# Routing places computed on GpSimd, and the channel product of the search rounds in rounded parts

## The chip, the cores and the metric

One core of a Trainium2 chip runs the whole kernel. The metric is the device time of one execution in microseconds (us). Engines are named as the profile names them: PE is TensorE, DVE VectorE, ACT ScalarE, POOL GpSimd, SP the queue that issues most plain DMAs. A semaphore is a counter; each engine works through its own instructions in order and waits where the program says so.

## What is computed

The input is 8192 tokens of 256 channels. Each is normalised (`xn`); then two branches are multiplied:

```python
s = rwkv(xn)      # k, v, r = mixes @ Wk, Wv, Wr; a recurrence over time; x += (sigmoid(r) * att) @ Wo
                  # kf = square(relu(xk2 @ WfkT)); s = x + sigmoid(xr2 @ WfrT) * (kf @ WfvT)
probs = softmax(xn @ Wg)                       # 8 experts
top_idx = top_k(probs.T, tokens // 8)          # each expert's 1024 tokens
expert = argmax over the experts that took the token, or over all if none did
g = silu(prob of the expert * gelu(xn @ W1[expert]) @ W2[expert])
out = x + s * g
```

`Wfv` is 1024 x 256: the second channel product `kf @ WfvT` sums over 8 chunks of 128.

## The kernel before

**Rounds.** The tokens go in 16 rounds (b = 0 to 15) of 512, four tiles (j) of 128. Round b runs three things woven together: the recurrence and the output projection of block b, the projections of block b + 1, and the channel mixing of block b - 1. Each engine has a written order, one function `round_` per engine; most rounds are hardware loops.

PE's round: `hidden(b - 1)` (8 chunks h into three PSUM banks, in rounded parts already: a high and a low part of weights and data in F32R, three products in place of one float32 product), `receptance(b - 1)`, `turn1(b + 1)`, `channel_out(b - 1, 0)`, `project_out(b)`, a routing step, `project(b + 1, 0, 1)`, `channel_out(b - 1, 1)`, `turn2(b)`, a routing step, `project(b + 1, 2)`, `channel_out(b - 1, 2)`, a routing step, `channel_out(b - 1, 3)`. `channel_out(b, j)` (line 961) is a tile's 8 products in float32, one per chunk, 128x128 weights from `kf2` and 256 columns of `wfv`:

```python
for h in range(HC):
    ins = pe.matmul(psKV[:, j // 2, ...], kf2[:, h, j * P:(j + 1) * P], wfv[:, h, :], start=(h == 0), stop=(h == HC - 1))
```

ACT's round (line 665): `logs`, `relu` and `square` of the first chunks (lines 642, 646), `shares(b)` (lines 626, 629; waits for DVE's `wkv_gap`), more `relu`, `norm1(b + 1)` (line 545, waits for POOL's `rstd1`), the last `relu` and `square`, `affine1`, `sigmoid_fr`, `take_kvr` in pieces (lines 590, 592), `norm2`, `affine2`, exponents, and `split_mix`, which makes `mix_hi`.

DVE's round: `wkv_state` (scans, line 1453), `embed_scale` and `embed_shift` of b + 1 (1558, 1563), routing point 0, `wkv_gap` (1460), `gate_out(b - 2)` (1542), `moments1(b + 1)` (1375, 1379), `residual2(b - 2)` (1549), `wkv_mix` (1471 to 1500), routing point 1, `mix1(b + 1)` (1392, 1396), `residual1(b)` (1533, waits for the output projection) with its statistics, point 2, `mix1_r`, `wkv_start` (1439 to 1447), point 3, `mix2` (1392, 1396, and 1431, which waits for `mix_hi`).

POOL's round: `rstd1(b + 1)` and `rstd2(b)`, four instructions on 128x4 each (lines 441 to 446), which turn variances into scales. `norm_scales` does the same for the first normalisation in rounds 0 to 3 (lines 409 to 425).

**Routing.** The logits and the softmax are made in rounds 0 to 3. In the search rounds 4 to 10 DVE looks bit by bit for each expert's threshold, four bits a round, one at each point (`try_bit`, lines 1210 to 1217: compare 128x512 and count; PE adds over partitions, line 837). Round 11 (`SELECT_ROUND`) counts ties, selects and chooses. In round 12 (`LIST_ROUND`), point 0, `place_tokens` (lines 1294 to 1347) turns the prefix sums (`win`), the counts (`psR`) and the one-hot choice (`pexp`), all 128x512, into a place for each token, and makes `expert_at`, the expert of each of the MLP's tiles. `routed` then frees SP, which loads W2 into the desk (a buffer whose upper part holds the routing tables; its lower 4096 words hold inputs of the router's rounds and nothing in the search rounds). SP then stores `s`, copies rows of x, loads the list, and W1.

**The list.** `list_part` (1354, 1355) copies 16 tiles' places and rows each round from 12 to 15, because the instruction in a loop needs fixed addresses, and `add_to_list` issues 16 indirect DMAs a round (line 434), eight behind `rstd1` and eight behind `rstd2` (all sixteen ahead of `rstd2` in round 15).

**The MLP.** 71 tiles of 128 tokens, each with its expert's weights; the second product is in rounded parts, 128x128 weights by 256 columns (lines 1062 to 1064). It starts about 826 us into the span.

## Time and profile before

| | us |
|---|---|
| median of 3 runs | 1076.61 (1076.31 to 1077.09) |
| the profiled execution | 1077.64 |
| its span, first to last instruction | 1075.8 |
| PE busy / DVE busy | 1015.7 / 882.0 |
| ACT busy / POOL busy | 689.6 / 383.4 |
| mean granted clock of PE | 0.981 |

Busy time is the union of an engine's records in the span. PE's records overlap, and their ends are modelled, so a spacing is read from starts. A float32 product has two records, a rounded one (F32R) one. A granted clock of 1 is 2.4 GHz and 0.5 is 1.2 GHz.

### The profile page before, as it was taken

Reading aid. Unit: us, or ns where it says so; the run is one execution under the profiler, and the core shown is the slowest. Engines: PE = TensorE matmul, PEld = TensorE weight load, DVE = VectorE, ACT = ScalarE, POOL = GpSimd, SP = SyncE. Lnnn points to the kernel's source line nnn. Section 1 sums busy time; section 2 is a strip of 40 time slices with the busy share of each in tenths; the row PEclk is TensorE's granted clock in tenths of the full one; section 3 lists DMA queues with packets and bytes.
Section 4 is the critical chain, followed back from the end, with each engine's and each line's share of the span. In section 5 each row is a group of like instructions: output and inputs, shape, how many; then the busy total and the mean of one; then the engine's idle time right before and its main releaser. Section 6 shows DMA issues by size and latency. Waiting matters only on the chain.

```text
span 1075.8 us, 18544 instructions
## 1 busy us (share of the span) xinstructions
PE 1015.7 (94%) x5410; PEld 832.7 (77%) x5410; DVE 882.0 (82%) x1763; ACT 689.6 (64%) x1231; POOL 383.4 (36%) x407
## 2 busy tenths in 40 slices
PE   4899999899999999999999969999999999999996
PEld 4578787677777767777776757777788999999996
DVE  5899898998988889898899987887665777777775
ACT  2558567585857658585765557595555666666663
POOL 3204055110101021010101045656762776666663
PEclk9889999999999999999999989999999999999998
DMA  7544320101102010110101020124361433333320
GB/s 257 168 141 120 98 79 20 40 7 54 58 0 58 0 58 15 43 58 0 58 0 59 1 59 1 59 68 129 120 223 40 122 122 114 113 114 109 108 67 21
DMA packets 59473, 80.28 MB, mean 75 GB/s; under 512 B 7678, under 2 KB 46719, under 8 KB 59394
## 3 DMA queue, kind: packets, MB, share of 16 engines
q1 hardware_dynamic: 48130, 54.16, 15.9%
q0 software_dynamic: 11280, 25.32, 7.9%
q8 instruction: 35, 0.57, 0.2%
q14 instruction: 28, 0.23, 0.1%
HBM read 64.38 MB, written 26.36 MB: 84 GB/s over the span
## 4 chain that ended last, share of the span: by engine, by line
PE 59%; DVE 19%; issue 9%; ACT 7%; POOL 4%; DMA 1%; DVEq 1%; SPq 0%; ACTq 0%; POOLq 0%
PE psKV L968 12%; PE psM L1042 11%; PE psM L905 11%; PE psM L919 5%; DVE arena L1453 2%; DVE arena L1396 2%; ACT arena L646 2%; PE psT L870 2%; ACT arena L545 2%; DVE bnst L1375 2%; PE psM L937 2%; PE psM L956 2%; PE psKV L1062 2%; POOL cf L444 2%; PE psKV L1064 1%
## 5 line engine op out<-in xcount | busy, mean ns | idle before, releaser
L968 PE MATMUL psKV<-arena 128*128 128x256 f32 x1024 | 231.2, 380 | 2.6 <-ACT arena L646 2.6
L968 PEld LDWEIGHTS psKV<-arena 128*128 128x128 f32 x1024 | 192.7, 190 | 42.0 <-issue 17.5
L441 POOL TENSOR_SCALAR lnw<-mv 128x4 f32<-128x4 f32 x32 | 19.0, 593 | 519.2 <-DVE mv L1379 519.2
L1042 PE MATMUL psM<-arena 128*128 128x128 f32 x1136 | 139.5, 276 | 1.5 <-DVE arena L1630 1.4
L1042 PEld LDWEIGHTS psM<-arena 128*128 128x128 f32 x1136 | 132.2, 192 | 3.2 <-DVE arena L1630 2.5
L937 PE MATMUL psM<-mix_hi,wfk_hi 128*128 128x512 f32 x256 | 107.8, 421 | 21.2 <-ACT arena L642 21.2
L592 ACT ACTIVATE arena<-psM 128x512 f32<-128x512 f32 x64 | 36.5, 588 | 127.9 <-PE psM L905 127.9
L1396 DVE SCALAR_TENSOR_TENSOR arena<-arena,vecs 128x512 f32<-128x512 f32 x160 | 109.9, 745 | 0.1
L507 POOL DMA_INDIRECT out_dram<-arena,list_sb x71 | 86.5, 1218 | 59.1 <-DVE arena L1661 50.4
L545 ACT ACTIVATE arena<-s_ring,cf 128x256 f32 (+1 forms) x128 | 66.4, 591 | 59.9 <-POOL cf L446 59.9
L939 PE MATMUL psM<-mix_hi,wfk_lo 128*128 128x512 f32 x256 | 102.3, 400 | 0.0
L642 ACT ACTIVATE arena<-psM 128x512 f32<-128x512 f32 x128 | 73.7, 587 | 28.9 <-PE psM L944 26.4
L768 ACT ACTIVATE arena<-psM 128x512 f32<-128x512 f32 x71 | 42.5, 599 | 63.2 <-PE psM L1042 63.2
L434 POOL DMA_INDIRECT sorted_list<-info_cur,place_cur x64 | 73.7, 1151 | 22.3 <-issue 20.6
L944 PE MATMUL psM<-mix_lo,wfk_hi 128*128 128x512 f32 x256 | 80.9, 398 | 0.0
L937 PEld LDWEIGHTS psM<-mix_hi,wfk_hi 128*128 128x128 f32 x256 | 49.7, 194 | 36.5 <-ACT arena L642 26.8
L646 ACT ACTIVATE arena<-arena 128x512 f32<-128x512 f32 x128 | 75.2, 624 | 1.0
L494 POOL DMA_INDIRECT arena<-xs_rows,list_sb x62 | 65.9, 1063 | 21.0 <-issue 18.6
L956 PE MATMUL psM<-arena 128*128 128x256 f32 x256 | 60.4, 383 | 4.6 <-ACT arena L642 4.6
L905 PE MATMUL psM<-arena,wk 128*128 128x512 f32 x128 | 61.5, 626 | 0.5 <-DVE arena L1396 0.5
L919 PE MATMUL psM<-wo,arena 128*128 128x256 f32 x256 | 59.4, 386 | 0.7 <-DVE arena L1500 0.5
L1392 DVE TENSOR_TENSOR arena<-arena 128x512 f32<-128x512 f32 x64 | 41.7, 688 | 22.0 <-ACT arena L553 21.9
(212 smaller groups left out, 2368.4 us busy)
## 6 DMA issues: line engine op xcount, KB each, us to landing
arena<-in_x SPq DMA_DIRECT2D x16, 512.0 KB, 4.1
desk<-in_xT SPq DMA_DIRECT2D x16, 512.0 KB, 4.1
xs_rows<-s_ring SPq DMA_DIRECT2D x16, 512.0 KB, 3.2
xs_rows<-in_x SPq DMA_DIRECT2D x16, 512.0 KB
desk<-in_x SPq DMA_DIRECT2D x15, 512.0 KB, 5.0
desk<-in_W SPq DMA_DIRECT2D x8, 512.0 KB, 8.4
arena<-in_W SPq DMA_DIRECT2D x8, 512.0 KB, 7.3
out_dram<-arena,list_sb POOLq DMA_INDIRECT x71, 2.7
```

The source lines that it names most:

```text
L507: pool.indirect_dma_start(out[:, :], bass.IndirectOffsetOnAxis(list_sb[:, t, 0:1], axis=0), out_t[i], None, bounds_check=T - 1, oob_is_err ...
L545: ins = act.activation(hn[:, j], xs[:, j * C:(j + 1) * C], ACT.Identity, scale=cf[:, 0, j:j + 1], bias=cf[:, 1, j:j + 1])
L646: act.activation(kf2[:, h], kf2[:, h], ACT.Square).then_inc(S["sq_done"], 1)
L905: ins = pe.matmul(psM[:, u % 3, :], w[:, k, c * P:(c + 1) * P], mixA[:, m, k, :], start=(k == 0), stop=(k == CH - 1))
L919: ins = pe.matmul(psM[:, 1 + j // 2, (j % 2) * C:(j % 2 + 1) * C], att[:, c, j * P:(j + 1) * P], wo[:, c, :], start=(c == 0), stop=(c == C ...
L937: pe.matmul(psM[:, h % 3, :], wfk_hi[:, k, n], mix_hi[:, k, :], start=(k == 0), stop=False)
L939: pe.matmul(psM[:, h % 3, :], wfk_lo[:, k, n], mix_hi[:, k, :], start=False, stop=False)
L944: ins = pe.matmul(psM[:, h % 3, :], wfk_hi[:, k, n], mix_lo[:, k, :], start=False, stop=(k == CH - 1))
L956: ins = pe.matmul(psM[:, (HC + u) % 3, (j % 2) * C:(j % 2 + 1) * C], mixB_r[:, k, j * P:(j + 1) * P], wfr[:, k, :], start=(k == 0), stop=( ...
L968: ins = pe.matmul(psKV[:, j // 2, (j % 2) * C:(j % 2 + 1) * C], kf2[:, h, j * P:(j + 1) * P], wfv[:, h, :], start=(h == 0), stop=(h == HC ...
L1042: ins = pe.matmul(psM[:, t % 2, f * P:(f + 1) * P], w1_t[t % 2][:, k, f * P:(f + 1) * P], xnT[t % 2][:, k, :], start=(k == 0), stop=(k == ...
L1396: return v.scalar_tensor_tensor(dst[:, c], dmix[:, c], vecs[:, c, V[m]:V[m] + 1], hT[:, c, 0:SEQ], ALU.mult, ALU.add)
```

## The change

Two things. The places are computed by four passes of POOL over 128x512 between DVE's steps, over the tables themselves; the list is scattered from `place` and `info` directly, in unrolled rounds; `expert_at` is made in round 14. And in rounds 4 to 11 `channel_out` becomes `channel_part`: by pairs of chunks p in place of tiles, from high and low parts. ACT makes `kf_hi` (two slots of two chunks, in the desk) and `wfv_hi`, POOL makes `kf_lo` and `wfv_lo` in the place of `kf2` and `wfv`. Ahead of round 12 POOL adds `wfv` together again. On ACT squares 4 to 7 move behind `affine1`.

POOL:

```diff
-            def add_to_list(b, half):
-
-                wait_run(pool, S["list_cur"], b - (LIST_ROUND - 1))
-                if isinstance(b, int) and b == LIST_ROUND:
...
+                for t in range(first, last):
+                    pool.indirect_dma_start(sorted_list[:, :], bass.IndirectOffsetOnAxis(place[:, t:t + 1], axis=0),
+                                            info[:, t, :].bitcast(I32), None).then_inc(S["list_scattered"], 16)
 
             def rstd(b, stats, mv, lnw, cf, step, ready):
 
...
+            def place_in_lists():
+
+                st = Steps(pool, S["place_step"], 4, 0, S["waited"])
+                pool.wait_ge(S["counts_kept"], 1)
+                pool.wait_ge(S["route_step"], R_KEPT)
+                st.then(pool.tensor_tensor(by_tile(before), by_tile(before), by_expert(counts), ALU.subtract))
+                pool.wait_ge(S["route_step"], R_STARTS)
+                st.wait()
+                st.then(pool.tensor_tensor(by_tile(before), by_tile(before), by_expert(work), ALU.add))
+                st.wait()
...
+                st.wait()
+                st.then(pool.tensor_tensor(before, before, chosen, ALU.mult))
+                st.end()
+
+            def take_lo(b, p):
+                wait_run(pool, S["kf_hi_done"], (b - BIT_ROUND) * J + (p + 1))
+                n, slot = slice(2 * p, 2 * p + 2), 2 * (p % 2)
+                pool.tensor_tensor(kf_lo[:, n], kf2[:, n], kf_hi[:, slot:slot + 2].bitcast(F32), ALU.subtract
...
+            def split_wfv():
+                pool.wait_ge(S["wfv_hi_done"], 1)
+                pool.wait_ge(S["kv_done"], J * ROUTER_ROUNDS)
+                pool.tensor_tensor(wfv_lo, wfv, wfv_hi.bitcast(F32), ALU.subtract).then_inc(S["wfv_lo_done"], 1)
+
+            def join_wfv():
+                pool.wait_ge(S["kv_done"], J * SELECT_ROUND)
+                pool.tensor_tensor(wfv, wfv_lo.bitcast(F32), wfv_hi.bitcast(F32), ALU.add).then_inc(S["wfv_whole"], 1)
+
+            def parts_round(b):
+                rstd1(b + 1)
+                take_lo(b, 0)
+                take_lo(b, 1)
+                rstd2(b)
+                take_lo(b, 2)
+                take_lo(b, 3)
+
+            def round_(b, mid=(0, 0), late=(0, 0), ahead=True):
                 if ahead:
                     rstd1(b + 1)
-                if listing:
-                    add_to_list(b, 0)
-                if not ahead:
-                    add_to_list(b, 1)
+                if isinstance(b, int) and b == LIST_ROUND:
+                    pool.wait_ge(S["pads_out"], 16)
+                    pool.wait_ge(S["route_step"], R_PLACED)
+                add_to_list(*mid)
                 rstd2(b)
                 if not ahead:
                     zero_rows()
-                if listing and ahead:
-                    add_to_list(b, 1)
+                add_to_list(*late)
 
...
-            norm_scales(ROUTER_ROUNDS + 1, NB - 4, NB - 1)
-            with pool.Fori(ROUTER_ROUNDS, LIST_ROUND) as b:
-                round_(b)
-            round_(LIST_ROUND, listing=True)
-            with pool.Fori(LIST_ROUND + 1, NB - 1) as b:
-                round_(b, listing=True)
-            round_(NB - 1, listing=True, ahead=False)
+            norm_scales(ROUTER_ROUNDS + 1, NB - 4, NB - 2)
+            norm_scales(ROUTER_ROUNDS + 2, NB - 1, NB - 1)
+            round_(ROUTER_ROUNDS)
+            split_wfv()
+            with pool.Fori(BIT_ROUND, LIST_ROUND) as b:
+                parts_round(b)
+            join_wfv()
+            place_in_lists()
+            round_(LIST_ROUND, mid=(0, 4), late=(4, 17))
+            round_(LIST_ROUND + 1, mid=(17, 26), late=(26, 39))
+            round_(LIST_ROUND + 2, mid=(39, 48), late=(48, 60))
+            round_(NB - 1, mid=(60, NTILE), ahead=False)
 
```

ACT:

```diff
+            def take_hi(b, p):
+                act.wait_ge(S["sq_done"], b * HC + (2 * p + 2))
+                act.wait_ge(S["kv_done"], b * J + (p - 1))
+                slot = 2 * (p % 2)
+                act.activation(kf_hi[:, slot:slot + 2], kf2[:, 2 * p:2 * p + 2], ACT.Copy).then_inc(S["kf_hi_done"], 1)
...
+            def split_wfv():
+                act.wait_ge(S["logits_done"], NB)
+                act.wait_ge(S["a_step"], 2 * NB)
+                act.activation(wfv_hi, wfv, ACT.Copy).then_inc(S["wfv_hi_done"], 1)
...
-            def round_(b, ffn=True, ahead=True, softmax=False, further=True):
+            def keep_counts():
+                act.wait_ge(S["route_pe"], 4)
+                act.activation(logits.rearrange("p (e t) -> p e t", e=E), psR[:].rearrange("p (t e) -> p e t", e=E),
...
                     relus(b - 1, 5)
+                if parts:
+                    take_hi(b - 1, 0)
                 if ahead:
                     norm1(b + 1)
                 if ffn:
                     relus(b - 1, 6)
                     squares(b - 1, 3)
                     relus(b - 1, 7)
-                    squares(b - 1, 4, 5, 6, 7)
+                    if not parts:
+                        squares(b - 1, 4, 5, 6, 7)
                 if softmax:
                     act.wait_ge(S["route_exp_in"], 1)
                     act.activation(probs, logits, ACT.Exp).then_inc(S["route_exp_out"], 1)
                 if ahead:
                     affine1(b + 1)
+                if softmax:
+                    split_wfv()
                 if isinstance(b, int) and b == 1:
                     keep_logits(2)
                 if ffn:
...
                     act.activation(wfk_hi[:], wfk, ACT.Copy).then_inc(S["wfk_hi_done"], 1)
+                if parts:
+                    squares(b - 1, 4, 5)
+                    take_hi(b - 1, 1)
                 if ahead:
                     take_kvr(b + 1, 0, 2)
                 if not ffn:
                     keep_logits(1)
+                if parts:
+                    squares(b - 1, 6, 7)
+                    take_hi(b - 1, 2)
                 norm2(b)
                 if ahead:
                     take_kvr(b + 1, 2, 4)
...
                 affine2(b)
                 if ahead:
                     exp_past(b + 1)
+                    if parts:
+                        take_hi(b - 1, 3)
                     take_kvr(b + 1, 4, 5)
                     exponents(b + 1)
                 split_mix(b, 0)
...
             round_(ROUTER_ROUNDS, softmax=True)
-            with act.Fori(BIT_ROUND, NB - 2) as b:
+            with act.Fori(BIT_ROUND, LIST_ROUND) as b:
+                round_(b, parts=True)
+            round_(LIST_ROUND, placing=True)
+            with act.Fori(LIST_ROUND + 1, NB - 2) as b:
                 round_(b)
             round_(NB - 2, further=False)
             round_(NB - 1, ahead=False)
```

PE:

```diff
-            def round_(b, extra, ffn=True, ahead=True):
+            def channel_part(b, p):
+                if p == 0:
+                    pe.wait_ge(S["wfv_lo_done"], 1)
+                    wait_run(pe, S["s_mult"], b)
+                done = b * J - (BIT_ROUND - 1) * J + (p + 1)
+                pe.wait_ge(S["kf_hi_done"], done)
+                out = lambda j: psKV[:, j // 2, (j % 2) * C:(j % 2 + 1) * C]
+                for j in range(J):
+                    for h in (2 * p, 2 * p + 1):
+                        hi = kf_hi[:, h % 4, j * P:(j + 1) * P]
+                        pe.matmul(out(j), hi, wfv_hi[:, h, :], start=(h == 0 and j % 2 == 0), stop=False)
+                        pe.matmul(out(j), hi, wfv_lo[:, h, :], start=False, stop=False)
+                pe.wait_ge(S["kf_lo_done"], done)
+                for j in range(J):
+                    for h in (2 * p, 2 * p + 1):
+                        ins = pe.matmul(out(j), kf_lo[:, h, j * P:(j + 1) * P], wfv_hi[:, h, :],
+                                        start=False, stop=(h == HC - 1 and j % 2 == 1))
+                ins.then_inc(S["kv_done"], 1)
+
+            def round_(b, extra, ffn=True, ahead=True, channel_out=channel_out):
                 if ffn:
                     hidden(b - 1, extra, b)
                     receptance(b - 1)
...
                 round_(b, router_point)
             round_(ROUTER_ROUNDS, softmax)
             with pe.Fori(BIT_ROUND, SELECT_ROUND) as b:
-                round_(b, sum_bit)
-            round_(SELECT_ROUND, route)
+                round_(b, sum_bit, channel_out=channel_part)
+            round_(SELECT_ROUND, route, channel_out=channel_part)
+            pe.wait_ge(S["wfv_whole"], 1)
             with pe.Fori(LIST_ROUND, NB - 1) as b:
                 round_(b, nothing)
             round_(NB - 1, nothing, ahead=False)
...
```

DVE (the eight lines of `place_tokens` from the reduction on stay):

```diff
                 elif point == 0:
+                    expert_starts()
+                elif point == 1:
                     place_tokens()
...
+            def expert_starts():
+                v.wait_ge(S["counts_kept"], 1)
+                R.then(v.tensor_tensor_scan(work, reset, logits, 0.0, ALU.mult, ALU.add))
+                R.wait()
+                R.then(v.tensor_scalar(starts(0).bitcast(I32), et(work)[:, :, NTILE - 1], float(P - 1), None, ALU.add))
+                R.wait()
+                R.then(v.tensor_scalar(starts(1).bitcast(I32), starts(0).bitcast(I32), 7, None, ALU.logical_shift_right))
+                R.wait()
+                R.then(v.tensor_copy(starts(2), starts(1).bitcast(I32)))
+                R.wait()
+                R.then(v.tensor_tensor_scan(starts(3), ones[:, 0:E], starts(2), 0.0, ALU.mult, ALU.add))
+                R.wait()
+                R.then(v.tensor_tensor(starts(4), starts(3), starts(2), ALU.subtract))
+                R.wait()
+                R.then(v.tensor_scalar(starts(5), starts(4), float(P), -1.0, ALU.mult, ALU.add))
...
-                R.then(v.tensor_tensor(work, work, logits, ALU.subtract))
-                R.wait()
-                R.then(v.tensor_tensor(et(work), et(work), c8(5).rearrange("p (e o) -> p e o", o=1).to_broadcast([P, E, NTILE]),
-                                       ALU.add))
-                R.wait()
-                R.then(v.tensor_tensor(te(win), te(win), work.rearrange("p (e t) -> p t e", e=E), ALU.add))
-                R.wait()
-                R.then(v.tensor_tensor(win, win, pexp, ALU.mult))
-                R.wait()
+                v.wait_ge(S["place_step"], 4)
...
                 R.then(v.tensor_scalar(info[:, :, 1:2].rearrange("p t o -> p (t o)"), gate, 0.5, None, ALU.mult))
+                R.wait()
+                assert R.k == R_PLACED, R.k
+
+            def tile_experts():
...
                 R.then(v.tensor_reduce(win[0:1, 0:NT], tw3, AX_X, ALU.add))
                 R.wait()
...
                 v.tensor_copy(tiny[:, 60:61], tiny[:, 0:1]).then_inc(S["routed"], 1)
                 R.end()
...
-            def list_part(b):
-
-                n = b - LIST_ROUND
-                if not (isinstance(b, int) and b == LIST_ROUND):
-                    wait_run(v, S["list_scattered"], n * (16 * LT))
-                v.tensor_copy(place_cur[:], place[:, ds(n * LT, LT)])
-                v.tensor_copy(info_cur[:].rearrange("p t w -> p (t w)"),
-                              info[:].rearrange("p t w -> p (t w)")[:, ds(n * (4 * LT), 4 * LT)].bitcast(I32)
-                              ).then_inc(S["list_cur"], 1)
-
             def listing(b, point):
-                if point == 0:
-                    list_part(b)
+                if point == 2 and isinstance(b, int) and b == NB - 2:
+                    tile_experts()
 
 
```

## Rows read from the trace of the kernel before

**Rows 1.** The page, part 1: busy us, share, instructions.

```profile
PE 1015.7 (94%) x5410; PEld 832.7 (77%) x5410; DVE 882.0 (82%) x1763; ACT 689.6 (64%) x1231; POOL 383.4 (36%) x407
```

**Rows 2.** Table by stretches: stretch: length, busy by engine, granted clock, DMA.

```profile
483.65:530.55 46.90, 45.41 (x192) 34.24 (x193) 41.23 (x86) 32.13 (x55) 5.47 (x8) 1.00 0.11 34
577.96:632.56 54.60, 44.56 (x169) 32.76 (x170) 51.81 (x99) 29.25 (x49) 7.09 (x10) 0.91 0.07 21
632.56:677.88 45.32, 44.27 (x185) 33.40 (x185) 36.33 (x64) 30.64 (x52) 24.67 (x25) 1.00 0.12 35
```

**Rows 3.** Waits of DVE, 202 to 578 us: total us, times, longest.

```profile
DVE s_ring L1533 <- PE psM L919: 14.1, 8, 2.0
DVE desk L1210 <- PE psR L837: 7.9, 8, 1.4
```

**Rows 4.** Chain of waits in the search rounds: start, us, what.

```profile
451.00 3.45 PE psKV L968 x16
```

**Rows 5.** Timeline of PE in the MLP: start, us, instruction.

```profile
899.77 0.28 PE L1062 MATMUL psR<-w_hi,hT_h 128*128 x1
...
900.72 0.28 PE L1064 MATMUL psR<-w_hi,hT_l 128*128 x1
```

**Rows 6.** Groups by line on ACT, 483.65 to 530.55 us: busy, mean ns | idle before.

```profile
L592 ACT ACTIVATE arena<-psM 128x512 f32<-128x512 f32 x4 | 2.2, 586 | 8.0 <-PE psM L905 8.0
...
L603 ACT ACTIVATE arena<-arena 128x1024 f32<-128x1024 f32 x1 | 1.1, 1052 | 0.0
```

**Rows 7.** Groups by line and shape on POOL, whole span.

```profile
L458 POOL MEMSET arena<- 128x512 f32 x9 | 4.2, 523 | 0.0
...
L413 POOL TENSOR_TENSOR desk<-desk,info 128x12 f32<-128x12 f32 x1 | 0.2, 223 | 0.1
...
L422 POOL TENSOR_TENSOR stats<-desk,info 128x4 f32<-128x4 f32 x1 | 0.2, 201 | 0.1
```

**Rows 8.** Timeline of DVE and POOL at 520 us.

```profile
520.22 1.22 DVE L1549 TENSOR_TENSOR s_ring<-s_ring,arena 128x1024 f32 x1
...
520.33 1.17 POOL L441 TENSOR_SCALAR lnw<-mv 128x4 f32<-128x4 f32 x1 [23.61 <-DVE mv L1379]
```

**Rows 9.** Single lines, whole span: count: ns min/median/max, first and last start.

```profile
L441 POOL TENSOR_SCALAR lnw<-mv x32: 192/385/1172, 19.5 to 779.1; 128x4 f32<-128x4 f32 x32
...
L442 POOL TENSOR_SCALAR lnw<-mv x32: 192/267/1667, 19.8 to 779.4; 128x4 f32<-128x4 f32 x32
...
L1630 DVE COPY arena<-arena x71: 681/685/885, 795.5 to 1058.4; 128x1024 f32 x71
...
L1396 DVE SCALAR_TENSOR_TENSOR arena<-arena,vecs x160: 718/746/754, 27.6 to 788.4; 128x512 f32<-128x512 f32 x160
```

**Rows 10.** Groups by line on DVE, 483.65 to 530.55 us.

```profile
L1217 DVE TENSOR_SCALAR_CACHE_REDUCE desk<-desk 128x512 f32<-128x512 f32 x4 | 3.0, 746 | 0.7 <-DVE desk L1215 0.7
L1375 DVE BATCH_NORM_STATS2 bnst<-s_ring 128x6 f32 x8 | 2.8, 415 | 0.1
```

**Rows 11.** Timeline of DVE in the placing round.

```profile
611.66 0.68 DVE L1297 COPY desk<-psR 128x512 f32<-128x512 f32 x1
...
618.02 0.69 DVE L1324 TENSOR_REDUCE desk<-desk 128x64 f32<-128x512 f32 x1
...
619.88 0.74 DVE L1339 TENSOR_TENSOR desk<-desk 1x576 f32<-1x576 f32 x1
...
621.89 1.28 DVE L1460 TENSOR_TENSOR arena<-arena 128x512 f32<-128x512 f32 x2
```

**Rows 12.** Timeline of PE in the placing round: idle before it in brackets.

```profile
627.07 0.80 PE L937 MATMUL psM<-mix_hi,wfk_hi 128*128 128x512 f32 x1 [10.03 <-ACT arena L642]
```

**Rows 13.** Table by stretches behind PE's idle time.

```profile
627.10:632.56 5.46, 5.46 (x13) 4.31 (x14) 5.46 (x10) 4.48 (x9) 4.43 (x6) 0.50 0.67 200
```

**Rows 14.** POOL: group of the list's issues, and timeline behind the last.

```profile
L434 POOL DMA_INDIRECT sorted_list<-info_cur,place_cur x64 | 73.7, 1151 | 22.3 <-issue 20.6
...
779.13 0.19 POOL L441 TENSOR_SCALAR lnw<-mv 128x4 f32<-128x4 f32 x1 [1.04 <-DVE mv L1379]
```

52 lines of the change are left out of this document (26 added, 26 removed).

## The prediction

> **What bounds the kernel now.** The page comes first: TensorE (PE) is busy 94% of the span, VectorE (DVE) 82%, ScalarE (ACT) 64%, GpSimd (POOL) 36% [rows 1]. Such shares mix stages, so the table by stretches is next. The search rounds, from one first channel product (`channel_out`, j = 0) to the next, repeat every 46.90 us with PE busy 45.41 and DVE 41.23. A round without routing work takes 45.32 with PE busy 44.27. The stretch of the select round and the placing takes 54.60 with PE busy only 44.56 at a mean granted clock of 0.91 and DVE busy 51.81 [rows 2]. So plain rounds are PE's; in a search round both engines are almost full; in the placing stretch DVE is the bound.
>
> How much of a search round's DVE is free? Its waits on other engines say it: over eight rounds 14.1 us for the output projection and 7.9 us for the bit's sum [rows 3], so 1.8 + 1.0 = 2.8 us per round. What DVE needs for itself is 46.9 - 2.8 = 44.1 us (41.2 busy, the rest dispatch between dependent instructions). PE needs 45.4. A change that takes work from PE can gain until DVE's 44.1 are reached, and anything over 2.8 us per round put on DVE lengthens the round.
>
> **The change, part by part.**
>
> *Channel product in parts, rounds 4 to 11.* Now a quarter of it is 16 records in 3.45 us (two for each of 8 products of 128x256) [rows 4]: 13.8 us per round. The new form is 96 single products with rounded operands. The MLP has that shape: eight steps from 899.77 to 900.72, 0.119 us each, weight load included [rows 5]. 96 x 0.119 = 11.4: PE gets 2.4 us shorter, to 43.0, below DVE's 44.1. Were nothing else changed, the round would fall to about 44.3, by 2.6 us.
>
> *ACT, per round.* `take_hi` adds four copies of 128x1024, 1.05 us each (nearest row, an Exp of that size) = 4.2 us. ACT waits 8.0 us per round for the projection [rows 6] and is busy 32.1 of 46.9 [rows 2]. The first copy lies ahead of `norm1`, where it waits for POOL's scales today. The second and third, with the squares moved there, lie around the first two `take_kvr`, where the 8.0 are. The fourth delays `exponents` and `split_mix` by 1.05, and DVE reaches `mix_lo` about when `mix_hi` ends today: up to 0.3 us. I take 0 to 0.3 per round. Without these gaps it would be 4.2.
>
> *POOL, per round.* `take_lo` adds four subtractions of 128x1024, both inputs in SBUF. No row has such a pass. Below: 512 words are written in 0.52 us by a memset [rows 7], 1.02 ns each; at that rate a pass of 1024 is 1.05. Above: undisturbed two-input operations take 0.201 us for 4 elements and 0.223 for 12 [rows 7], 2.75 ns an element, so 3.0. I take two streams read one after the other at the memset's rate, 1024 x 2 x 1.02 = 2.1 us. GPSIMD Engine Reference of the Trainium skill (section 3.1) gives 4497 ns for an add of 2048, which would make it 2.25; no run here has shown it.
>
> POOL itself has the time (5.5 of 46.9 busy [rows 2]), and by the order on the engines PE asks for each low part 5 to 10 us after its high part is made. What counts is DVE. A POOL instruction on 4 elements takes 0.192 us at its shortest and 1.172 at its longest [rows 9]; a long one begins at 520.33 inside a DVE add of two SBUF operands (520.22 for 1.22) and ends 0.06 behind it [rows 8]. POOL waits for the rest of DVE's whole instruction. Does it hold the other way too? A DVE copy of 128x1024 takes 0.685 at the median and up to 0.885 beside POOL's issues, but `mix` never more than 0.754 against 0.746 in 160 [rows 9]: the reads of POOL have been too small to tell. I take it that it does, for the pass's whole 2.1 us: the wait seen is for a complete instruction, and that is a lock and not a shared rate.
>
> The Trainium skill states that lock for both sides: SBUF — State Buffer, section Who interferes with whom, says that a DVE instruction with two SBUF inputs and a POOL instruction that reads SBUF exclude each other, and that whichever issues first keeps the port to its end. The rows above agree for one direction. By that rule the sum is the one below; by the `mix` row alone (DVE never held) it would be rival one's.
>
> Not all of DVE competes: statistics (2.8), the counting pass (3.0) [rows 10], the two operations with a PSUM operand and small ones leave about 10 of 44 us free of it. So a pass costs DVE 0.77 x 2.1 = 1.6, four 6.5. Round: 44.1 + 6.5 = 50.6, +3.7. Seven steady rounds: **+26**. In round 11 DVE has no slack to give: **+6.5**; PE's saving there gains nothing.
>
> *Splitting the weights.* `split_wfv`: 2048 wide, 4.2 us on POOL at the start of round 4, beside scans of DVE: 0.77 x 4.2 = **+3** (bounds 0 and 5.6); the copy on ACT, twice 1.05, is in its gap.
>
> *Joining them and placing, round 12.* Today the placing runs from 611.66 to 621.89 on DVE, ahead of `wkv_gap` [rows 11]; ACT stands in `shares` behind it and PE idles 10.03 us for the next `relu` [rows 12], then runs 5.5 us at a granted clock of 0.50, its lower level, 1.2 GHz [rows 13]: 2.7 lost. After, point 0 keeps the scan and six small ones, 1.2 + 6 x 0.2, so 2.5 us at most: 7.7 less. Of these, the part from the reduction at 618.02 to 619.88 returns behind `wkv_mix` (1.9), the tiles' experts up to 621.89 in round 14 (2.0), where DVE has 36.3 of 45.3 busy [rows 2]. The counts' copy goes to ACT (0.6, ahead of `relu`: nothing). But `join_wfv`, 2048 wide, may start only when round 11's last product is done, and PE waits for it before its next instruction: 4.2 us of PE idle, and DVE held at its scans for 0.77 x 4.2 = 3.2. The four placing passes of 512 (1.05 each) hold DVE another 3, about half ahead of `wkv_gap`. DVE reaches the gap 7.7 - 3.2 - 1.5 = 3.0 earlier, and some of the clock's loss goes with it, less what the first norm behind these passes on POOL is late. **-3** (bounds -8, with DVE never held, and +4, where the join delays all).
>
> *The list.* 64 issues stay, 1.15 us each [rows 14]. The two small copies per round and the wait for landed parts go; in round 15 twelve issues fewer lie ahead of `rstd2`. POOL idles 1.04 us between its last issue and that norm today [rows 14], so this gives nothing. `routed` comes in round 14 instead of 12. SP waits for it in order, with W2's loads, a store of `s`, five copies of x, the list's load and W1's behind it; SP gets there only after its loop, in round 14, so it is late by less than half a round, and W2 is first read behind round 15's hidden product: 0. The list's own load waits for the last scatter as before. `norm_scales` of the last block is split, one short set more on POOL, idle there: 0.
>
> Sum: 26 + 6.5 + 3 - 3 = **+32** on the profiled execution's 1077.64, its span of 1075.8 plus 1.8 around it: 1109.6. The median of the runs is 1.0 lower: **1109 us**. With passes of 1.05 it is 44.1 + 3.2 = 47.3, +0.4 x 7 + 3.2 + 1.6 - 5 = +3: 1079. With passes of 3.0 that all meet a competing instruction, 44.1 + 12 = 56.1, +9.2 x 7 + 12 + 6 + 4 = +86: 1163. Both ends need every unknown at once; I take 1083 to 1132 as the forecast's own range.
>
> **Rivals.** *One: DVE is not held* (for: the `mix` row; against: the wait for a whole instruction, [rows 8, 9]). Then seven rounds gain 2.6 (18), round 11 nothing, the placing 6 to 8: 1076.6 - 25 = 1052, from 1048 to 1060. It ends on the other side. The point that decides is the hold of one pass: at 2.8 / (4 x 0.77) = 0.9 us the round is as long as before. Chance 0.33.
> *Two: POOL loses every contest*, and the low parts come late. DVE keeps 44.1, but PE waits at `kf_lo`; the fourth part has the least room, 5 us. A wait of 2 to 3 us per round gives back what PE saved: 1070 to 1090, say 1077. For it: another small POOL instruction has taken 1.667 us [rows 9], more than any one DVE instruction beside it. Against: the wait at 520.33 ended at the next boundary [rows 8]. Chance 0.08.
> *Three: the parts don't save PE time* (with operands that alternate, steps nearer 0.144, where 96 take 13.8) while DVE is held as forecast: 1113, inside the forecast's range, chance 0.04.
> The forecast itself has 0.55.
>
> **How the numbers follow.** About 0.2% (2 us) is what this measurement can tell from no change. Slower: the forecast and three 0.59, less 0.02 for its low end, and 0.04 of rival two, 0.61. Faster: rival one and 0.02 of rival two, 0.35. The same: 0.04. To hold eight in ten the range has to reach from rival one's middle to the forecast's upper end: 1050 to 1130.
>
> **What would show it.** Right: in the search rounds DVE's two-input instructions (`mix`, scans of 1.2 us) with records or gaps of 2 to 3 us wherever POOL has a `take_lo`, rounds of about 50 us, PE busy about 43 of them, DVE never waiting for the output projection. PE idle 4 us at the head of round 12. Wrong: `mix` still 0.75 beside POOL's passes and rounds of 44 to 45 us; or POOL's passes at 1 us; or PE waiting for POOL at the parts.

## The result, and the profile after

| | before | after |
|---|---|---|
| median, us (lowest to highest) | 1076.46 (1075.79 to 1077.09) | 1120.62 (1120.22 to 1121.17) |
| span of the profiled execution | 1075.8 | 1119.2 |
| mean granted clock | 0.981 | 0.969 |

The medians are of 4 runs each. The ratio is 1.041 [1.039, 1.043]: 44 us slower. The forecast was 1109, 32 us slower, with 1050 to 1130 as the range. That range reaches from 26 us faster to 54 us slower; the forecast's own 1083 to 1132 is the narrower test, and it holds the result too.

The first part of the page after the change, to be read against [rows 1]:

```profile
PE 1016.1 (91%) x5666; PEld 835.0 (75%) x5666; DVE 951.9 (85%) x1750; ACT 720.4 (64%) x1265; POOL 493.0 (44%) x455
```

DVE is busy 70 us longer on work that has fewer instructions than before (1750 in place of 1763). PE is busy as long as before, though its products became fewer microseconds. Both need the stages. Here are stretches of the changed kernel, each from the start of one `residual2` on DVE to the next: a search round, the select round with the join and the placing, and the round behind it.

```profile
core 0: us, PE busy (x) PEld busy (x) DVE busy (x) ACT busy (x) POOL busy (x), PEclk, DMA share, GB/s
502.34:554.74 52.40, 45.65 (x224) 34.54 (x224) 49.62 (x87) 35.81 (x59) 16.72 (x12) 0.97 0.10 30
607.73:671.89 64.16, 49.60 (x225) 37.15 (x226) 63.37 (x88) 37.99 (x62) 26.94 (x17) 0.92 0.08 25
671.89:715.75 43.86, 42.23 (x176) 31.61 (x176) 38.28 (x73) 28.71 (x50) 27.51 (x25) 1.00 0.13 37
```

The search round went from 46.90 to 52.40 us and DVE from 41.2 to 49.6 busy. The starts of `residual2` in the rounds split the difference between the two spans, 43.4 us:

| from the `residual2` of one round to that of another | before | after | difference |
|---|---|---|---|
| round 2 to 3 | 50.76 | 48.83 | -1.9 |
| 3 to 4 (with `split_wfv`) | 46.35 | 50.09 | +3.7 |
| 4 to 11, seven search rounds | 328.90 | 367.49 | +38.6 |
| 11 to 12 (last parts, join, placing) | 58.20 | 64.16 | +6.0 |
| 12 to 13 | 45.98 | 43.86 | -2.1 |
| 13 to the end | 403.9 | 403.5 | -0.4 |

The rows add up to +43.9; ahead of round 2 the changed kernel gains another 0.4.

**What stretches DVE.** The timeline of the changed kernel in one search round, POOL's four `take_lo` (line 484) and the DVE records beside them. Columns: start, duration, engine, line, operation, tiles, shapes, and how many instructions the row joins.

```profile
506.53 3.32 POOL L484 TENSOR_TENSOR kf_lo<-arena,kf_hi 128x1024 fp32r<-128x1024 f32 x1
517.08 2.69 POOL L484 TENSOR_TENSOR kf_lo<-arena,kf_hi 128x1024 fp32r<-128x1024 f32 x1 [7.23 <-ACT kf_hi L699]
528.32 2.44 POOL L484 TENSOR_TENSOR kf_lo<-arena,kf_hi 128x1024 fp32r<-128x1024 f32 x1 [0.42 <-ACT kf_hi L699]
537.25 2.83 POOL L484 TENSOR_TENSOR kf_lo<-arena,kf_hi 128x1024 fp32r<-128x1024 f32 x1 [6.48 <-ACT kf_hi L699]
...
507.61 3.39 DVE L1567 SCALAR_TENSOR_TENSOR arena<-arena 128x512 f32<-128x512 f32 x2
517.48 4.82 DVE L1480 SCALAR_TENSOR_TENSOR arena<-arena,vecs 128x512 f32<-128x512 f32 x4
528.43 4.53 DVE L1523 TENSOR_TENSOR_SCAN arena<-wneg,arena 128x512 f32<-128x512 f32 x2
537.73 4.89 DVE L1480 SCALAR_TENSOR_TENSOR arena<-arena,vecs 128x512 f32<-128x512 f32 x4
```

Beside no pass, the same rows take 1.28 (line 1567, two instructions), 2.73 (line 1480, four) and 2.33 (the scans, two). The differences are 2.11, 2.09, 2.20 and 2.16: one DVE instruction in each row stood still for about 2.1 us. So it is with all 32 passes of rounds 4 to 11: each held one DVE instruction with two SBUF inputs. Which one changes from round to round: a scan (lines 1562, 1523), `mix` (1480) or one of the operations beside them (1567, 1476, 1527), in round 11 also one of the selection. One line's own statistics say it too: minimum, median, maximum.

```profile
L1480 DVE SCALAR_TENSOR_TENSOR arena<-arena,vecs x160: 720/745/2899, 27.0 to 832.1; 128x512 f32<-128x512 f32 x160
```

Before, `mix` never took more than 0.754 [rows 9]. With 4 x 2.14 = 8.6 taken off, the round is 43.8, DVE's own need (44.1 in the prediction).

**Who waits now.** The waits of DVE, then of PE, in the search rounds after the change (202 to 606): who, for whom, in total, times, the longest.

```profile
DVE desk L1311 <- PE psR L918: 1.4, 1, 1.4
DVE s_ring L1617 <- PE psM L1000: 0.4, 1, 0.4
```

```profile
PE psM L1018 <- ACT arena L689: 23.8, 14, 3.2
PE psM L986 <- DVE arena L1480: 16.6, 7, 2.6
```

DVE's 14.1 us for the output projection and 7.9 for the bit's sum [rows 3] are gone: 0.4 and 1.4, once each, is all that it still waits for PE. PE waits for `mix`, and for the `relu` on ACT that stands behind DVE's work. Such a wait costs PE twice, as idle time and as a slower clock behind it. PE's timeline at the end of one:

```profile
499.18 0.40 PE L1018 MATMUL psM<-mix_hi,wfk_hi 128*128 128x512 f32 x1
499.42 0.40 PE L1020 MATMUL psM<-mix_hi,wfk_lo 128*128 128x512 f32 x1
...
503.17 0.65 PE L1018 MATMUL psM<-mix_hi,wfk_hi 128*128 128x512 f32 x1 [2.90 <-ACT arena L689]
503.62 0.63 PE L1020 MATMUL psM<-mix_hi,wfk_lo 128*128 128x512 f32 x1
504.04 0.63 PE L1018 MATMUL psM<-mix_hi,wfk_hi 128*128 128x512 f32 x1
```

Ahead of the idle 2.90 us the starts are 0.23 apart, behind it 0.43, until 506.6: the granted clock went from its upper level (2.4 GHz) to its lower one (1.2 GHz). That is why PE is busy 45.65 in this round, not the 43.0 forecast. PE being late, though, moved nothing here, as DVE was later still.

**The weights' split and join.** The timeline of the changed kernel around `split_wfv` (line 490), and around `join_wfv` (line 494):

```profile
229.54 5.18 POOL L490 TENSOR_TENSOR wfv_lo<-arena,wfv_hi 128x2048 fp32r<-128x2048 f32 x1 [17.03 <-PE psKV L1049]
...
230.51 4.23 DVE L1314 TENSOR_TENSOR desk<-desk 128x1 f32<-128x1 f32 x1
234.89 0.16 DVE L1316 TENSOR_TENSOR desk<-desk 128x1 int32<-128x1 int32 x1
```

```profile
652.16 4.88 POOL L494 TENSOR_TENSOR arena<-wfv_lo,wfv_hi 128x2048 f32<-128x2048 f32 x1 [1.35 <-PE psKV L1068]
...
652.61 5.59 DVE L1515 TENSOR_TENSOR mix_lo<-arena,mix_hi 128x512 fp32r<-128x512 f32 x2
...
657.64 0.77 PE L1018 MATMUL psM<-mix_hi,wfk_hi 128*128 128x512 f32 x1 [5.56 <-POOL arena L494]
```

The split shows the hold at its purest: a DVE operation on one element per partition (two inputs, both in SBUF), 0.159 us at the median of its 29 occurrences, took 4.23 and ended at 234.74, where POOL's pass ended (234.72). The join held `mix_lo` for 5.59 - 1.28 = 4.3 us and PE for 5.56.

### The profile page after: what moved, and what is told of

Read it like the earlier page. It is cut to its first block, busy times and chain, and to the rows that moved or that the text cites. A ratio compares the mean times of both kernels' runs of the same rounds, so it can differ in the third digit from the quotient of the medians.

```text
span 1119.2 us, 19095 instructions
## 1 busy us (share of the span) xinstructions
PE 1016.1 (91%) x5666; PEld 835.0 (75%) x5666; DVE 951.9 (85%) x1750; ACT 720.4 (64%) x1265; POOL 493.0 (44%) x455
## 4 chain that ended last, share of the span: by engine, by line
PE 51%; DVE 27%; issue 12%; ACT 5%; POOL 3%; DVEq 1%; DMA 1%; SPq 0%; ACTq 0%; POOLq 0%
PE psM L1143 11%; PE psKV L1049 7%; PE psM L986 6%; DVE arena L1480 5%; PE psM L1000 4%; PE psM L1037 3%; DVE bnst L1459 2%; DVE arena L1537 2%; PE psM L1018 2%; PE psM L1025 2%; PE psM L1020 2%; DVE arena L1523 2%; PE psKV L1163 1%; PE psKV L1165 1%; PE psKV L1164 1%
## 5 line engine op out<-in xcount | busy, mean ns | idle before, releaser
L484 POOL TENSOR_TENSOR kf_lo<-arena,kf_hi 128x1024 fp32r<-128x1024 f32 x32 | 91.8, 2870 | 122.1 <-ACT kf_hi L699 122.1
L1480 DVE SCALAR_TENSOR_TENSOR arena<-arena,vecs 128x512 f32<-128x512 f32 x160 | 139.6, 930 | 0.1
L1049 PE MATMUL psKV<-arena 128*128 128x256 f32 x512 | 114.5, 380 | 0.5 <-ACT arena L693 0.5
L1049 PEld LDWEIGHTS psKV<-arena 128*128 128x128 f32 x512 | 96.8, 190 | 18.7 <-issue 6.3
L1020 PE MATMUL psM<-mix_hi,wfk_lo 128*128 128x512 f32 x256 | 105.9, 414 | 0.0
L438 POOL DMA_INDIRECT sorted_list<-info,place x64 | 74.3, 1161 | 28.3 <-issue 18.5
L986 PE MATMUL psM<-arena,wk 128*128 128x512 f32 x128 | 68.1, 677 | 19.9 <-DVE arena L1480 19.1
L1025 PE MATMUL psM<-mix_lo,wfk_hi 128*128 128x512 f32 x256 | 84.4, 412 | 1.1 <-DVE mix_lo L1515 1.1
L600 ACT ACTIVATE arena<-psT,vecs 128x512 f32<-128x512 f32 x64 | 46.2, 772 | 39.1 <-PE psT L951 35.5
L1063 PE MATMUL psKV<-wfv_hi,kf_hi 128*128 128x256 f32 x256 | 69.8, 313 | 0.0
```

The source lines that it names most:

```text
L438: pool.indirect_dma_start(sorted_list[:, :], bass.IndirectOffsetOnAxis(place[:, t:t + 1], axis=0), info[:, t, :].bitcast(I32), None).then_ ...
L484: pool.tensor_tensor(kf_lo[:, n], kf2[:, n], kf_hi[:, slot:slot + 2].bitcast(F32), ALU.subtract).then_inc(S["kf_lo_done"], 1)
L986: ins = pe.matmul(psM[:, u % 3, :], w[:, k, c * P:(c + 1) * P], mixA[:, m, k, :], start=(k == 0), stop=(k == CH - 1))
L1020: pe.matmul(psM[:, h % 3, :], wfk_lo[:, k, n], mix_hi[:, k, :], start=False, stop=False)
L1025: ins = pe.matmul(psM[:, h % 3, :], wfk_hi[:, k, n], mix_lo[:, k, :], start=False, stop=(k == CH - 1))
L1049: ins = pe.matmul(psKV[:, j // 2, (j % 2) * C:(j % 2 + 1) * C], kf2[:, h, j * P:(j + 1) * P], wfv[:, h, :], start=(h == 0), stop=(h == HC ...
```

## The experiments

The first four ran on one chip (the kernel before: 1076.21), the next three on a second and the last three on a third, where the kernel before takes 1090.08 and 1088.93. The stretch behind the last `residual2` takes 267 to 269 us on these two and 254 on the first. So ratios and round lengths are compared between chips, not totals, and an expected total is read as its ratio to the 1076.5 that it was worked out from.

**Placing on its own.** The change without the parts: `round_` in place of `parts_round`, no split, no join, `channel_out` in every round.

```diff
-            split_wfv()
             with pool.Fori(BIT_ROUND, LIST_ROUND) as b:
-                parts_round(b)
-            join_wfv()
+                round_(b)
```

> The changed kernel with only its first half: places on POOL, the list from the tables, the split norm_scales; the channel product stays in float32 in all rounds. Theory (a POOL pass that reads SBUF holds DVE's two-input instructions for about 2.1 us per 1024 words): search rounds back at 46.9, nothing to join, and the placing gives what the chain of before promised: 7.7 us less ahead of wkv_gap, less some 1.5 to 3 of hold by the four passes of 512, and 2.4 from the split norm_scales: 1064 to 1070 us. Rival (the placing itself costs, the first norm being late on POOL behind it): 1074 or more.

Measured: 1065.31, ratio 0.989 [0.988, 0.991]. The placing part is a gain of 11 us, and the parts cost 55.

```profile
423.41:470.31 46.90, 45.40 (x194) 34.23 (x193) 41.23 (x87) 32.15 (x55) 5.48 (x8) 1.00 0.11 34
564.75:617.83 53.08, 47.75 (x197) 35.08 (x196) 50.68 (x89) 34.35 (x59) 12.56 (x12) 0.99 0.10 30
617.83:662.19 44.36, 44.36 (x176) 33.54 (x177) 38.26 (x73) 28.77 (x50) 27.51 (x25) 0.94 0.13 37
```

These are stretches of this kernel. The total is in the 1064 to 1070 expected. The search round is the old one to the hundredth; the select and placing stretch is 5.1 us shorter than the old 58.20, and the next 1.6. Against the same stretch of the full change (64.16, DVE 63.37) DVE is 12.7 less busy, about four holds (8.6) and the join's (4.3).

**Splitting `norm_scales` on its own**, in the kernel before.

```diff
-            norm_scales(ROUTER_ROUNDS + 1, NB - 4, NB - 1)
+            norm_scales(ROUTER_ROUNDS + 1, NB - 4, NB - 2)
+            norm_scales(ROUTER_ROUNDS + 2, NB - 1, NB - 1)
```

> The kernel before with norm_scales of the last block split off, nothing else. Theory: round 3 of the changed kernel began 2.4 us earlier than before because of this alone: 1074 us (1073.5 to 1075). Rival (the 2.4 us come from the weights' copy or from the other order on ACT): 1076.5.

Measured: 1074.13, ratio 0.9987 [0.9976, 0.9997]; the stretch from the `residual2` of round 2 to that of round 3 is 48.84 in place of 50.76. The prediction had put this edit at nothing; it gives 2 us, as this run's expectation had it. Where it comes from is one DVE row, before and with the edit (line 1171 is line 1170 of the kernel before):

```profile
186.40 0.69 DVE L1170 TENSOR_TENSOR desk<-desk,info 128x512 f32<-128x512 f32 x1 [2.92 <-POOL info L425]
183.60 0.69 DVE L1171 TENSOR_TENSOR desk<-desk,info 128x512 f32<-128x512 f32 x1 [0.93 <-POOL info L425]
```

DVE multiplies the logits by the scales and waits for POOL's last ones. Split, POOL does three quarters of that set in time that was idle before, and DVE waits 2.0 us less.

**The write alone**: a memset of the same words in place of `take_lo`. PE's third product is taken from the high part, so the low part of the data is left out of the result.

```diff
-                pool.tensor_tensor(kf_lo[:, n], kf2[:, n], kf_hi[:, slot:slot + 2].bitcast(F32), ALU.subtract
-                                   ).then_inc(S["kf_lo_done"], 1)
+                pool.memset(kf2[:, n], 0.0).then_inc(S["kf_lo_done"], 1)
```

> The changed kernel with take_lo a memset of the same 1024 words (written, nothing read), and PE's third product taken from the high part, so that the low part of kf is left out of the result; all waits, copies of ACT and PE's products stay. Theory (POOL's reads hold DVE): rounds of 44.3 to 45.5 us in place of 52.4, DVE's mix at 0.75 again: 1120.6 - 7 x 7.5 - 8.5 = 1060 (1055 to 1068). Rival (the rounds are long because of the order: ACT's four copies, the moved squares, PE waiting at the parts): over 50 us per round, above 1100.

Measured: 1062.63, ratio 0.987 [0.986, 0.989], rounds of 44.65, the later ones of 45.49, in each of which DVE waits 0.8 for the output projection. The group of these passes, then a round of this kernel:

```profile
L484 POOL MEMSET arena<- 128x1024 f32 x32 | 30.5, 952 | 142.7 <-ACT kf_hi L698 142.7
```

```profile
418.30:463.79 45.49, 42.66 (x224) 33.41 (x224) 41.41 (x86) 35.63 (x59) 9.21 (x12) 1.00 0.11 35
```

DVE's 41.4 is what it was before (41.2). So in the search rounds ACT's copies, PE's new products and POOL's writes lengthen nothing; the loss there goes with what the passes read.

**The subtractions on DVE**: POOL does none, DVE does all four at its routing points.

```diff
+                if parts:
+                    take_lo(b, 0)
```

(and so for 1, 2 and 3, with `v.tensor_tensor` in place of `pool.tensor_tensor`)

> The changed kernel with the four take_lo of a round done by DVE itself (1.22 us each by its rows of that size), at the places where POOL's passes would have been ready. Theory (a POOL pass costs DVE its read time, 2.1 us, more than the same work on DVE): rounds of 44.1 + 4.9 = 49.0 to 49.5: 1120.6 - 7 x 3.1 - 3.5 = 1095 (1090 to 1100). Rival (DVE is slowed only because it is full, POOL's pass takes work from it that it would otherwise do): the same or longer than the changed kernel, 1120 to 1135.

Measured: 1102.29, ratio 1.024 [1.020, 1.028], above the 1095 expected and outside its range; rounds of 49.5, but for three of 51.2 to 51.9. DVE is busy 45.6 a round, 4.4 more than before. The expectation had left out a wait of PE for the low parts, here from 240 to 540:

```profile
PE psKV L1064 <- DVE kf_lo L1655: 19.2, 12, 2.2
```

Two of a round's four parts come late in this way, and DVE waits in turn for the output projection, up to 2.8 us at a time. Even so, DVE doing the work itself is 18 us faster than DVE held while POOL does it.

**Two passes beside instructions that don't compete.** `take_lo` 0 waits for `gap_done`, 1 for `o_done` and `mix1_done`; `take_hi` 0 moves ahead of `shares`.

```diff
-                rstd1(b + 1)
+                wait_run(pool, S["gap_done"], b * CH + CH)
                 take_lo(b, 0)
+                rstd1(b + 1)
+                wait_run(pool, S["o_done"], b + 1)
+                wait_run(pool, S["mix1_done"], 2 * b + 4)
                 take_lo(b, 1)
```

> The changed kernel with take_lo 0 and 1 of each search round moved: pass 0 waits for gap_done, so that it lies beside gate_out (a PSUM operand) and the block's statistics, pass 1 waits for o_done and mix1_done, so that it lies beside residual1 (a PSUM operand), its statistics and the counting pass. Passes 2 and 3 stay, nothing is left out, and POOL's work is the same. If a pass holds DVE only where DVE's instruction reads two SBUF tensors, two of four holds of 2.1 us go: a round of 52.4 - 4.2 = 48.2, eight rounds 33 less, about 1087 (1080 to 1094), with no long statistics records. If any POOL pass holds any DVE instruction, or if the work as such counts, it stays at 1115 to 1121, with the long records on other lines.

Measured: ratio 1.017 [1.015, 1.020] against 1.041: about 26 of the 33 us expected, just outside the range (1.003 to 1.016 as a ratio). The timeline has POOL's two moved passes first, then DVE: beside the pass at 454.60, beside one that was left in place (469.82), and beside the pass at 484.12:

```profile
454.60 2.37 POOL L484 TENSOR_TENSOR kf_lo<-arena,kf_hi 128x1024 fp32r<-128x1024 f32 x1 [13.55 <-PE psM L1003]
...
484.12 2.37 POOL L484 TENSOR_TENSOR kf_lo<-arena,kf_hi 128x1024 fp32r<-128x1024 f32 x1 [11.96 <-DVE arena L1547]
...
454.34 1.22 DVE L1620 TENSOR_TENSOR s_ring<-s_ring,psM 128x1024 f32 x1 [1.56 <-PE psM L1003]
455.70 1.40 DVE L1462 BATCH_NORM_STATS2 bnst<-s_ring 128x6 f32 x4
...
469.82 4.88 DVE L1483 SCALAR_TENSOR_TENSOR arena<-arena,vecs 128x512 f32<-128x512 f32 x4
...
483.69 1.21 DVE L1629 SCALAR_TENSOR_TENSOR arena<-arena,psKV 128x1024 f32<-128x1024 f32 x1
484.82 1.40 DVE L1462 BATCH_NORM_STATS2 bnst<-s_ring 128x6 f32 x4
```

Statistics and the operations with a PSUM operand keep their 1.40 and 1.2 us beside a pass, while `mix` beside a pass still takes 4.88. So the hold depends on what DVE reads. Why less came back is in the first DVE row: a wait of 1.56 for the output projection. Rounds are 49.03 or 50.00, not 48.2, and DVE's wait in them is 0.8 or 1.6, the whole difference but for 0.2. The mean granted clock is 0.97 in the shorter and 0.93 in the longer ones; behind PE's idle time at a longer round's start (busy 3.3 of 5 us) it is 0.58:

```profile
436.00:441.00 5.00, 3.27 (x8) 2.59 (x9) 4.76 (x12) 3.17 (x6) 4.13 (x5) 0.58 0.31 100
```

Here PE's idle time and its lower clock do reach the end, because DVE is no longer the later of the two.

**One input in place of two.** POOL multiplies `kf2` by 0 in place; the low part of the data is left out of the second channel product.

```diff
-                pool.tensor_tensor(kf_lo[:, n], kf2[:, n], kf_hi[:, slot:slot + 2].bitcast(F32), ALU.subtract
-                                   ).then_inc(S["kf_lo_done"], 1)
+                pool.tensor_scalar(kf_lo[:, n], kf2[:, n], 0.0, None, ALU.mult).then_inc(S["kf_lo_done"], 1)
```

> The changed kernel with take_lo as a pass with one input (kf2 times 0, written in place; the low part of the data is left out of the second channel product). It reads one stream of 1024 words where the subtraction reads two. If a hold lasts for the reading of the streams, it is 1.05 in place of 2.1 us: a round of 44.1 + 4 x 1.05 = 48.3, eight rounds 33 less, 1084 to 1092. If a hold has a fixed price for each pass, whatever it reads: 1115 to 1121. If a pass with one input does not hold DVE at all: rounds of 44.7, 1058 to 1064, as with the write alone.

Measured: ratio 1.002 [1.0005, 1.003], rounds of 47.05 to 47.09 but for the first (47.31) and the last (47.69). That is below all that was expected (1084 to 1092 is 1.007 to 1.014). Two of a round's passes and the DVE rows beside them:

```profile
489.05 2.83 POOL L484 TENSOR_SCALAR kf_lo<-arena 128x1024 fp32r<-128x1024 f32 x1 [6.88 <-ACT kf_hi L698]
...
498.72 2.82 POOL L484 TENSOR_SCALAR kf_lo<-arena 128x1024 fp32r<-128x1024 f32 x1 [0.43 <-ACT kf_hi L698]
...
489.17 3.51 DVE L1479 SCALAR_TENSOR_TENSOR arena<-arena,vecs 128x512 f32<-128x512 f32 x4
...
498.81 3.18 DVE L1522 TENSOR_TENSOR_SCAN arena<-wneg,arena 128x512 f32<-128x512 f32 x2
```

The hold is 3.51 - 2.73 = 0.78 and 3.18 - 2.33 = 0.85: 0.8 us a pass, and 43.8 + 4 x 0.8 = 47.0 is the round. A price of 2.1 for any pass is out. The surprise is that the pass itself got longer, 2.82 where the subtraction takes 2.37 undisturbed, and DVE worked beside it for 2 of those 2.8 us. The `mix` row taken apart shows the instruction that was held and one behind it, inside the same pass:

```profile
489.17 1.52 DVE L1479 SCALAR_TENSOR_TENSOR arena<-arena,vecs 128x512 f32<-128x512 f32 x1
490.61 0.74 DVE L1479 SCALAR_TENSOR_TENSOR arena<-arena,vecs 128x512 f32<-128x512 f32 x1
```

Only the first two-input instruction is held; the next ones run at their own length while the pass goes on. This pass differs from the subtraction in its operation as well as in its inputs, and no run separates the two.

**Twice the passes, half as wide.** Each `take_lo` as two passes of 128x512.

```diff
-                pool.tensor_tensor(kf_lo[:, n], kf2[:, n], kf_hi[:, slot:slot + 2].bitcast(F32), ALU.subtract
+                pool.tensor_tensor(kf_lo[:, 2 * p], kf2[:, 2 * p], kf_hi[:, slot].bitcast(F32), ALU.subtract)
+                pool.tensor_tensor(kf_lo[:, 2 * p + 1], kf2[:, 2 * p + 1], kf_hi[:, slot + 1].bitcast(F32), ALU.subtract
                                    ).then_inc(S["kf_lo_done"], 1)
```

> The changed kernel with each take_lo as two passes of 128x512 in place of one of 128x1024: the same words, twice the passes. If the hold goes with the words that POOL reads, each piece holds DVE 1.05 us and a round stays at 52.4, ratio 1.041 (up to 1.045, for the second start of POOL). If a pass has a fixed part, as the placing passes of 512 words suggest, which held DVE 1.3 us each, it is 2 x 1.3 in place of 2.1: a round of 54.4 and a ratio of 1.055. If DVE gets in between the pieces and the second one then falls on an instruction that does not compete, rounds get shorter, 51 or less.

Measured: ratio 1.039 [1.038, 1.041], rounds of 52.21. One pair of pieces and the two DVE rows that they fell on:

```profile
504.38 1.98 POOL L484 TENSOR_TENSOR kf_lo<-arena,kf_hi 128x512 fp32r<-128x512 f32 x1 [0.19 <-ACT kf_hi L700]
506.33 2.19 POOL L485 TENSOR_TENSOR kf_lo<-arena,kf_hi 128x512 fp32r<-128x512 f32 x1
...
504.06 3.38 DVE L1563 TENSOR_TENSOR_SCAN arena<-arena 128x512 f32<-128x512 f32 x2
507.37 2.30 DVE L1568 SCALAR_TENSOR_TENSOR arena<-arena 128x512 f32<-128x512 f32 x2
```

3.38 - 2.33 = 1.05 and 2.30 - 1.28 = 1.02: the two engines took turns, and the price went with the words. A fixed part of a pass isn't seen here. The placing passes of 512 words do cost more: in `place_only` a subtraction of DVE beside one takes 2.05 in place of 0.69, a hold of 1.36. They read their tables in another order, by tile and by expert; whether that is the reason no run shows.

**The join as a write.** A memset of the same 128x2048 words; from round 12 on the weights of the second channel product are zero, and the addition is left out.

```diff
-                pool.tensor_tensor(wfv, wfv_lo.bitcast(F32), wfv_hi.bitcast(F32), ALU.add).then_inc(S["wfv_whole"], 1)
+                pool.memset(wfv, 0.0).then_inc(S["wfv_whole"], 1)
```

> The changed kernel with the join ahead of round 12 as a memset of the same 128x2048 words (the weights of the second channel product from round 12 on are zero: the addition is left out). POOL then reads nothing: about 1.9 us in place of 4.9, and DVE's mix_lo at that place back from 5.6 to 1.3. If the join was in the way of both engines, 3 to 5 us go: round 11 to 12 of 59 to 61 in place of 64.2, a ratio to the kernel before of 1.036 to 1.038. If DVE, late by its four holds, sets that round anyway, only what PE loses at a lower clock comes back, under 1 us: 1.040 or 1.041.

Measured: ratio 1.0385 [1.037, 1.040]; the stretch from the `residual2` of round 11 to that of round 12 is 59.80 in place of 64.16. `mix_lo` (652.15, 1.28 us) is back at its length. So the join's 4.4 us are DVE's hold of 4.3. PE still waits 2.47 for the memset, and nothing is lost by it. The ratio lies just above the 1.036 to 1.038 expected, and its interval reaches up to 1.040, so it is the stretch in the trace that decides.

**Half of the parts.** The placing as changed; parts for chunks 0 to 3 only, both passes in the two places found above; chunks 4 to 7 stay float32. The low weights of four chunks fit into the desk, so nothing is joined.

```diff
-                pool.tensor_tensor(wfv_lo, wfv, wfv_hi.bitcast(F32), ALU.subtract).then_inc(S["wfv_lo_done"], 1)
+                pool.tensor_tensor(wfv_lo, wfv[:, 0:4], wfv_hi.bitcast(F32), ALU.subtract).then_inc(S["wfv_lo_done"], 1)
...
-            join_wfv()
```

> The placing as in the changed kernel, and the parts of the channel product for chunks 0 to 3 only, with both POOL passes beside DVE instructions that do not compete; chunks 4 to 7 stay float32. The low weights of four chunks lie in the desk, so that nothing has to be joined ahead of round 12. PE saves half of 2.4 us a round, and DVE needs its 44.1 to 45: rounds of 45.0 to 45.5 in place of 46.9, eight of them 11 less than the placing part alone at 1065.3: 1054 (1050 to 1062). If passes in those stretches hold DVE all the same (2 x 2.1 us), rounds of 48 and 1074 or more.

Measured: ratio 0.984 [0.982, 0.987], where the placing part alone has 0.989, and in the range expected (1050 to 1062 is 0.975 to 0.987); rounds of 45.36 to 46.06. In the rounds of 46.06 the first pass was late and reached into `residual2`, which takes 1.23 otherwise:

```profile
464.68 2.13 DVE L1633 TENSOR_TENSOR s_ring<-s_ring,arena 128x1024 f32 x1
```

**The first pass earlier.** `take_hi` 0 ahead of the third `relu` in place of behind it.

```diff
-                    relus(b - 1, 2)
+                    if not parts:
+                        relus(b - 1, 2)
                 if parts:
                     take_hi(b - 1, 0)
+                    relus(b - 1, 2)
```

> Parts for chunks 0 to 3 only, as before, with the first high part of a round made ahead of the third relu of its round in place of behind it. It then ends about 0.6 us earlier, and POOL's pass beside the statistics ends about when residual2 begins, where it held it for 0.9 us in the rounds of 46.06. Rounds of 45.3 to 45.6, eight of them 4 to 6 us less: a ratio to the kernel before of 0.979 to 0.981 against 0.984 with the late pass. If PE's work sets the round by now, or the third relu comes too late for it, there is no gain: 0.984 or more.

Measured: ratio 0.982 [0.981, 0.983], rounds of 45.59. The pass came earlier, but not early enough:

```profile
461.49 2.41 POOL L484 TENSOR_TENSOR kf_lo<-arena,kf_hi 128x1024 fp32r<-128x1024 f32 x1 [21.07 <-ACT kf_hi L694]
...
463.32 1.66 DVE L1635 TENSOR_TENSOR s_ring<-s_ring,arena 128x1024 f32 x1
```

`residual2` is still held for 0.4, and the ratio is a little above the 0.979 to 0.981 expected, its interval reaching into them. The intervals of this run and of the one with the late pass overlap, so that this order is better rests on the rounds (45.59 against 46.06). This version beats both kernels: 1.8% faster than the one before on the same chip.

## Why the prediction was right, and where it was short

The direction and the mechanism held: POOL's passes hold DVE, and DVE sets the round. Of 44 us, 32 were forecast. By its own steps:

- **The length of a hold, 2.1 us, was right**: 2.09 to 2.20 in a search round, 1.02 and 1.05 for half the words. The step that led to a hold was sound too: a tiny POOL operation had waited inside a DVE add [rows 8], and the lock works in the other direction as well. That the size came out at 2.1 is partly luck. It was worked out as two streams, each read at the memset's rate, and by that a one-input pass would hold for 1.05; it holds for 0.8. The record of the subtraction is 2.37 where nothing disturbs it, longer than the prediction's 2.1 and 2.25. The Trainium skill (SBUF — State Buffer, Who interferes with whom) says that the one which issues first keeps the port to its end. The traces agree for the two-input pass: the one-element operation of 0.16 us took 4.23, and ended with the pass. They agree too that a POOL instruction that only writes leaves DVE alone (write_only), as does a DVE instruction with one SBUF input (free_windows). They don't agree for a pass with one input: 0.8 us of its 2.8.
- **The discount of 0.77 failed.** It took the passes to fall at random over DVE's round, of which 10 in 44 us are free of competition. They don't: each pass waits for a high part, and ACT makes that part at a set place in its order. In every round all four held an instruction with two SBUF inputs. Nor is a share of free time the chance of a free pass: a pass of 2.4 us has to fit into a free stretch whole, and one that reached out of it by 1 us cost 0.9 (`half_parts`). A round has 4 x 2.14 = 8.6 of hold. Less the slack, 46.9 - 43.8 = 3.1 by the trace, that is +5.5, where the prediction had 6.5 less 2.8 = +3.7; without the discount its own numbers give 8.4 less 2.8 = +5.6. Seven rounds gave 38.6 against 26, and this term is the 12 us that the forecast was short; what was off in the others nearly cancels. `free_windows` shows the other side of it: with a wait ahead of each, two of the four fell where nothing is lost.
- **PE's saving was right and of no use.** 24 products are made in 2.9 us, so 96 in 11.7 (11.4 forecast), and PE is busy 43.1 in the rounds of `lo_one_input` that are at a full clock (43.0 forecast). In the changed kernel it is 45.65, with a granted clock of 0.97. That PE, now the one that waits, loses clock was not in the sum; it cost nothing there, since DVE is later. In `free_windows`, PE's idle time and lower clock together made the rounds up to 1.8 us longer than the 48.2 of DVE's need and two holds.
- **Round 11**: +6.5 forecast. By `place_only` the parts cost that stretch 64.16 - 53.08 = 11.1: the join's hold of 4.4 and 6.7 for four holds, some of which its little slack took.
- **The split**: 3 forecast, 3.7 measured, with a hold of 4.1 on one instruction. Against `place_only`, where this stretch takes 45.27, it is 4.8. The discount was wrong here in the same way.
- **Joining and placing, -3 forecast**: the parts of it were -5.1 and -1.6 for the placing (about -6 forecast ahead of the join) and +4.4 for the join (+3.2), together -2.3. PE's 5.56 idle behind the join is covered by DVE's lateness.
- **`norm_scales` split, 0 forecast, -1.9 measured.** The prediction looked at POOL's idle time, not at who stood behind the last scales in that round: DVE, which waited 2.92 for them and now waits 0.93.
- **The list**: nothing, as forecast. From the `residual2` of round 13 on, the kernels differ by 0.4 us.

The sum of the measured steps: -1.9 + 3.7 + 38.6 + 6.0 - 2.1 - 0.4 = +43.9. Rival one (DVE not held) fell with the first timeline, and write_only shows what it would have been: 1063. Rival two fell with PE's waits, of which none in the search rounds names `kf_lo`. Rival three fell with the products' starts, 0.118 apart (14 of them from 512.45 to 513.98) and not 0.144.

What stays open: why a pass with one input holds DVE for 0.8 us only and yet lasts 2.8; why the placing passes hold it longer per word; and whether all four passes of a round could be put in free places, for which `write_only` (0.987, with no hold in the search rounds but those of split and join left) is the nearest measure.
